# A turn's last twelve probability blocks: from TensorE's transposes to VectorE's 32x32 squares and a way through HBM

## The chip, the core and the metric

The kernel runs on one core of one Trainium2 chip. The metric is the device time of one execution in microseconds; the kernel before was timed in three runs. One further execution was taken with the hardware profiler, and every row below comes from it.

## The reference

One transformer layer with adaptive normalisation, for two sequences of 1024 tokens and 256 features, all in float32:

```
mod = silu(c) @ wmod                                   # shift, gain and gate for both halves
h   = layernorm(x) * (1 + ca) + sa
x   = x + ga * attention(h)       # 16 query heads, 4 key/value heads, 128 features, causal
h   = layernorm(x) * (1 + cb) + sb
x   = x + gb * ffn(h)             # gated (silu), weights behind Walsh-Hadamard transforms
```

Inside the attention: `scores = q k^T / sqrt(128)`, masked where a key lies behind its query, a softmax over the keys, `out = probabilities @ v`, and a projection back to 256 features that is summed over the heads.

## The kernel before

**Two numbers for one.** Every float32 matrix that goes into a matmul is split into a high and a low part, and a product is three matmuls (high x high, high x low, low x high; the helper `three`, L971 to L973). ScalarE makes the high part from PSUM, VectorE subtracts it from the same PSUM bank to get the low part.

**Turns, rows, units.** The attention runs in 8 turns (2 sequences x 4 key/value heads). In a turn there are 8 query rows of 128 tokens, each with 4 heads. Row i needs keys 0 to i, thus i + 1 key blocks of 128. One key block of one row, over the four heads, is a *unit*: 36 in a turn. Rows are paired in four windows of nine units, (7, 0), (6, 1), (5, 2), (4, 3).

**One unit.** `T`: TensorE transposes the probabilities of four heads, 128x128 each, into half of a PSUM tensor (L1097, two such halves); ScalarE copies them to `pt_hi` (L644), VectorE writes `pt_lo` (L869), three slots each. `V`: two units later TensorE multiplies them with the values into the row's output bank (L971 to L973 with `pt_hi`, `pt_lo`, `v_hi`, `v_lo`).

**One row of scores.** `S`, for a row and a head: three matmul passes (L1082, L1085, L1088) into one of two score tensors; VectorE adds the mask and takes the row maximum (L865); ScalarE takes the exponential, with its sum (L619); GpSimd inverts the sum (L511) and scales the row (L514). The scores of a window are made between the units of the window before it, so a row is complete in SBUF several units ahead of its first transpose. TensorE may write a score tensor again when the exponential of two heads before is done.

**The order.** There is no scheduler: `walk()` writes one list of steps, and every engine goes through that list and does its own share, in order. Semaphores order the engines among themselves. Steps besides `T`, `V` and `S` are `C` (a projection chunk of the next turn's q, k, v, in the last window), `Y` (a finished row through the output projection, and VectorE's addition to x, L879), `VT` (the values transposed), `LF`, `LN`, `L`, `LH`, `LL` (the second layer norm of 256 tokens, in the second window), `W` and `WP` (GpSimd's splitting of weights), `B` (butterflies of the down weights, on GpSimd, last turn) and `GB` (the second gate, VectorE, second turn). The projected row of the last window ends inside the next turn.

**DMA.** SP issues all large transfers from one queue, in program order: the weights of each turn (`w_raw`, L422, and `wp_raw`, L413), which wait until the former ones have been split, and at the start the down weights into `raw_down` (L418), which lie there unused until the last turn.

After the attention the feed-forward part runs to the end, with its own loop. The change does not touch it beyond its buffers.

## Time and profile before

| | us |
|---|---|
| median of 3 runs (lowest, highest) | 958.68 (958.41, 958.84) |
| the profiled execution | 958.28 |
| its span, first to last instruction | 956.1 |

| engine | busy us | share of the span | instructions |
|---|---|---|---|
| TensorE, matmuls | 937.3 | 98% | 5504 |
| TensorE, weight loads | 822.0 | 86% | 5504 |
| VectorE | 646.9 | 68% | 1313 |
| ScalarE | 509.1 | 53% | 1062 |
| GpSimd | 455.5 | 48% | 596 |

The span and what lies around it (2.2 us) make the profiled execution's own time. Matmuls are pipelined and a matmul's end is modelled, so the busy time of TensorE is an upper figure; the distance between the starts of neighbours is the safer measure. Idle time of an engine costs only where another one waits for it. Lines are those of the kernel before.

### The profile page before, as it was taken

What the parts mean: (1) busy time and instruction counts of PE and PEld (TensorE: products, weight loads), DVE (VectorE), ACT (ScalarE), POOL (GpSimd) and SP (SyncE); (2) the same over time, 40 slices, a digit from 0 to 9 for tenths busy, and PEclk for the clock granted to TensorE, in tenths of its full rate; (3) what the DMA queues carried; (4) which work ended last, traced back from release to release, by engine and by line L of the source; (5) the groups of instructions that cost most, each with busy time, mean ns of one, the idle gap of its engine ahead of it and who ended that gap; (6) DMA issues with size and microseconds to landing.
All of it is one profiled execution on the core that took longest, in us unless ns stands there. A gap on an engine that the chain in (4) does not pass through costs nothing.

```text
span 956.1 us, 14857 instructions
## 1 busy us (share of the span) xinstructions
PE 937.3 (98%) x5504; PEld 822.0 (86%) x5504; DVE 646.9 (68%) x1313; ACT 509.1 (53%) x1062; POOL 455.5 (48%) x596
## 2 busy tenths in 40 slices
PE   6999999999999999999999999999999999999997
PEld 5889889988998899889888898889888987888887
DVE  5677657766786577657765787478747876874554
ACT  3366556655665566546654666466546665321111
POOL 1466627662766175717670767076707674120000
PEclk9999999999999999999999999999999999999999
DMA  8000100000000000100000000000000011000000
GB/s 316 23 1 2 34 1 23 1 34 1 23 2 34 1 23 1 34 1 23 2 34 1 24 1 34 1 23 2 1 1 1 1 46 55 1 2 22 22 22 22
DMA packets 9603, 21.28 MB, mean 22 GB/s; under 512 B 1216, under 2 KB 5568, under 8 KB 9408
## 3 DMA queue, kind: packets, MB, share of 16 engines
q1 hardware_dynamic: 8816, 20.19, 6.2%
q8 instruction: 41, 0.67, 0.3%
q10 hardware_dynamic: 720, 0.21, 0.1%
q14 instruction: 26, 0.21, 0.1%
HBM read 18.30 MB, written 2.10 MB: 21 GB/s over the span
## 4 chain that ended last, share of the span: by engine, by line
PE 88%; DVE 6%; ACT 4%; DMA 1%; issue 1%; SPq 0%; POOL 0%; DVEq 0%; ACTq 0%; POOLq 0%
PE ps L971 19%; PE ps L973 18%; PE ps L972 18%; PE ps L1097 11%; PE ps L1082 6%; PE ps L1088 6%; PE ps L1085 6%; DVE ps L865 3%; ACT prob L619 2%; DVE pt_lo L869 2%; ACT pt_hi L644 1%; PE ps L995 1%; DMA w_raw<-in_wqkv 1%; PE ps L1051 1%; PE ps L1142 1%
## 5 line engine op out<-in xcount | busy, mean ns | idle before, releaser
L511 POOL TENSOR_TENSOR rinv<-rsum,mone 128x1 f32<-128x1 f32 x256 | 142.8, 558 | 264.8 <-ACT prob L619 264.7
L869 DVE TENSOR_TENSOR pt_lo<-ps,pt_hi 128x512 fp32r<-128x512 f32 x288 | 198.1, 688 | 63.9 <-ACT pt_hi L644 62.1
L644 ACT ACTIVATE pt_hi<-ps 128x512 fp32r<-128x512 f32 x288 | 170.9, 596 | 128.2 <-PE ps L1097 127.3
L619 ACT ACTIVATE prob<-ps,nmax 128x1024 f32<-128x1024 f32 (+7 forms) x256 | 189.7, 741 | 84.8 <-DVE nmax L865 84.0
L865 DVE CUSTOM_DVE_ANT_0 ps<-ps,mask_f 128x1024 f32<-128x1024 f32 (+7 forms) x256 | 193.7, 763 | 46.7 <-PE ps L1088 44.9
L514 POOL TENSOR_SCALAR prob<-prob,rinv 128x1024 f32<-128x1024 f32 (+7 forms) x256 | 191.3, 747 | 54.0 <-POOL rinv L511 54.0
L1097 PE MATMUL ps<-ident,prob 128*128 128x128 f32 x1152 | 172.0, 273 | 0.9 <-POOL prob L514 0.2
L1097 PEld LDWEIGHTS ps<-ident,prob 128*128 128x128 f32 x1152 | 140.9, 140 | 22.8 <-DVE pt_lo L869 2.1
L971 PE MATMUL ps<-pt_hi,v_hi 128*128 128x512 f32 x288 | 134.3, 466 | 0.0
L1082 PE MATMUL ps<-k_hi,q_hi 128*128 128x512 f32 (+4 forms) x384 | 112.7, 347 | 2.7 <-ACT prob L619 2.7
L973 PE MATMUL ps<-pt_hi,v_lo 128*128 128x512 f32 x288 | 113.7, 395 | 0.0
L972 PE MATMUL ps<-pt_lo,v_hi 128*128 128x512 f32 x288 | 113.5, 394 | 0.0
L1088 PE MATMUL ps<-k_hi,q_lo 128*128 128x512 f32 (+4 forms) x384 | 110.6, 342 | 0.0
L1085 PE MATMUL ps<-k_lo,q_hi 128*128 128x512 f32 (+4 forms) x384 | 110.4, 342 | 0.0
L821 DVE SCALAR_TENSOR_TENSOR q_lo<-ps,q_hi 128x512 fp32r<-128x512 f32 x64 | 44.1, 691 | 61.3 <-ACT q_hi L608 61.3
L1082 PEld LDWEIGHTS ps<-k_hi,q_hi 128*128 128x128 f32 x384 | 69.5, 189 | 15.8 <-ACT prob L619 3.5
L971 PE MATMUL ps<-h_hi,w_hi 128*128 128x512 f32 x192 | 78.9, 411 | 2.9 <-DVE h_lo L757 2.9
L608 ACT ACTIVATE q_hi<-ps 128x512 fp32r<-128x512 f32 x64 | 38.3, 598 | 73.4 <-PE ps L973 73.4
L1085 PEld LDWEIGHTS ps<-k_lo,q_hi 128*128 128x128 f32 x384 | 70.7, 188 | 7.7
L973 PE MATMUL ps<-h_hi,w_lo 128*128 128x512 f32 x192 | 75.9, 395 | 0.0
L972 PE MATMUL ps<-h_lo,w_hi 128*128 128x512 f32 x192 | 75.7, 394 | 0.0
L1088 PEld LDWEIGHTS ps<-k_hi,q_lo 128*128 128x128 f32 x384 | 70.4, 188 | 5.2
(137 smaller groups left out, 1685.9 us busy)
## 6 DMA issues: line engine op xcount, KB each, us to landing
w_raw<-in_wqkv SPq DMA_DIRECT2D x8, 768.0 KB, 4.2
wp_raw<-in_wproj SPq DMA_DIRECT2D x8, 512.0 KB, 3.5
prob<-in_wug SPq DMA_DIRECT2D x4, 512.0 KB, 4.6
out_y<-prob SPq DMA_DIRECT2D x8, 256.0 KB, 2.2
x<-in_x SPq DMA_DIRECT2D x3, 512.0 KB, 12.4
prob<-in_wmod SPq DMA_DIRECT2D x1, 1024.0 KB, 10.2
raw_down<-in_wdn SPq DMA_DIRECT2D x1, 1024.0 KB, 13.7
x<-in_x SPq DMA_DIRECT2D x2, 256.0 KB, 4.0
```

The costliest lines, as they stand in the source:

```text
L514: g_.tensor_scalar(row(i, h), row(i, h), rinv[:, at, h:h + 1], 1.0, ALU.mult, ALU.mult).then_inc(prob_done, 1)
L619: a_.activation(row(i, h).rearrange("p (a n) -> p a n", a=nb), score_banks(i, h).rearrange("p (a n) -> p a n", a=nb)[:, :, 0:w], ACT.Exp, ...
L644: a_.activation(pt_hi[:, n % 3, :], ring(t, "T", n), ACT.Copy).then_inc(pth_done, 1)
L865: v_.tensor_tensor_reduce(scores, scores, late, -1.0, 3.0e38, ALU.add, ALU.min, nmax[:, place(n), h:h + 1]).then_inc(max_done, 1)
L869: v_.tensor_tensor(pt_lo[:, n % 3, :], ring(t, "T", n), pt_hi[:, n % 3, :].bitcast(F32), ALU.subtract).then_inc(ptl_done, 1)
L971: mm(dst, w_h, r_h, start=start, stop=False)
L972: mm(dst, w_h, r_l, start=False, stop=False)
L973: return mm(dst, w_l, r_h, start=False, stop=stop)
L1082: mm(dst[:, a * CH:a * CH + wide], q_hi[:, h, q_at], k_hi[:, a * w:a * w + wide], start=True, stop=False)
L1085: mm(dst[:, a * CH:a * CH + wide], q_hi[:, h, q_at], k_lo[:, a * w:a * w + wide], start=False, stop=False)
L1088: last = mm(dst[:, a * CH:a * CH + wide], q_lo[:, h, q_at], k_hi[:, a * w:a * w + wide], start=False, stop=True)
L1097: last = tr(ring(t, "T", n)[:, q * P:(q + 1) * P], row(i, q, j * P, (j + 1) * P), ident[:, :])
```

## The change

Twelve of a full turn's 36 units are no longer transposed by TensorE. They are the last ones of the large rows: key blocks 5 to 7 of row 7, 3 to 6 of row 6, 3 to 5 of row 5, 3 and 4 of row 4. In the last turn only the seven of rows 7 and 6 are moved.

For a moved row there are three new steps:

- `X`, per head: VectorE transposes each 32x32 square of the row's last blocks where it stands, from `prob` into a new tile `blocks` (a STREAM_TRANSPOSE of 128 partitions x 384, 512, 384 or 256 columns).
- After the fourth head SP stores `blocks` in HBM (`spill`, two slots), waits for that, and loads it back in four transfers of 32 partitions into `raw_down`, so that the squares land in their transposed places. `raw_down` holds one row's group: the load waits until the last low part of the former group is made.
- `E`, per unit: ScalarE copies the unit from `raw_down` to `pt_hi`, VectorE writes `pt_lo`, both one unit ahead of where the transpose stood. `V` is as before.

`pt_hi` and `pt_lo` get a fourth slot; the small and the large row of a window are interleaved in another order (`ORDER`), so that moved and transposed units mix; the down weights are loaded in the last turn instead of at the start, and both butterflies stand in the last window. The butterflies' tiles share memory with `blocks`. The splitting of high and low parts stays with ScalarE and VectorE.

```diff
+ORDER = ("bbbsbbxxx", "bbbsxsxxx", "bbbssxsxx", "bbbssxssx")
...
+def moved(t, n):
+    return n in MOVED and (t + 1 < TURNS or UNITS[n][0] > 5)
...
+        turns7 = [(t, "X", NT - 1, h) for h in range(QPG)]
+        out += rest[:1] + [(t, "VT", 0, 0)] + (turns7[2:3] if t else []) + s0[3 if t else 0:] + ([s6[0]] if t else []) + rest[1:]
+        out += [(t, "WP", 0, 0)] + turns7[3:] if t else []
...
+            if t + 1 < TURNS and 0 < p + 1 < NW or t + 1 == TURNS and p == 0:
+                for h, k in enumerate((3, 4, 5, 7) if p == 0 < t else (4, 5, 6, 8) if p == 0 else (3, 4, 5, 6)):
+                    squares[k].append((t, "X", WINDOWS[p + 1][0], h))
+            elif t + 1 < TURNS:
+                squares[7].append((t + 1, "X", NT - 1, 0))
+                squares[8].append((t + 1, "X", NT - 1, 1))
...
+                if n + 1 < NU and moved(t, n + 1):
+                    out.append((t, "E", n + 1, 0))
+                out += extra[:1] + ([] if moved(t, n) else [(t, "T", n, 0)]) + extra[1:]
...
+            def swap_blocks(t, i):
+                g, size = GROUPS.index((t, i)), len(group_units(i))
+                sp.wait_ge(block_done, squared(t, i, QPG - 1))
+                sp.dma_start(spill[g % 2, :, 0:size * CH], blocks[:, 0:size * CH]).then_inc(spill_s[g % 2], 16)
+                sp.wait_ge(*spilled(t, i))
+                if g:
+                    t_of, i_of = GROUPS[g - 1]
+                    sp.wait_ge(el_done, max(entered(t_of, n) for n in MOVED if UNITS[n][0] == i_of))
+                for kb in range(NB):
+                    sp.dma_start(raw_down[kb * QB:(kb + 1) * QB, 0:size * CH].rearrange("p (a n) -> p a n", a=NB),
+                                 spill[g % 2, :, kb * size * P:(kb + 1) * size * P].rearrange(
+                                     "(a p) n -> p a n", a=NB)).then_inc(swap_s[g % 2], 16)
...
+                if what == "E":          # ScalarE
+                    act.wait_ge(pv_done, this(pv_done, t, n - 3))
+                    act.wait_ge(*landed(t, UNITS[n][0]))
+                    a_.activation(by_head(pt_hi, n), swapped_tile(n), ACT.Copy).then_inc(eh_done, 1)
...
+                if what == "E":          # VectorE
+                    dve.wait_ge(eh_done, entered(t, n))
+                    v_.tensor_tensor(by_head(pt_lo, n), swapped_tile(n), by_head(pt_hi, n).bitcast(F32),
+                                     ALU.subtract).then_inc(el_done, 1)
+                if what == "X":
+                    if h == 0 and g:
+                        dve.wait_ge(*spilled(*GROUPS[g - 1]))
+                    dve.wait_ge(prob_done, this(prob_done, t, scored(n, h)))
+                    v_.transpose(blocks[:, 0:len(mine) * CH].rearrange("p (k j h q) -> p j k h q", k=NB, j=len(mine), h=QPG)[:, :, :, h, :],
+                                 row(n, h, mine[0] * P, (n + 1) * P).rearrange("p (j k q) -> p j k q", j=len(mine), k=NB)
+                                 ).then_inc(block_done, 1)
```

The order of VectorE in the first window of the fifth turn, from the low part of the fourth transposed unit on, before (L869 low part, L865 a row maximum, here of row 1's heads, L874 low part of a finished output, L879 addition to x):

```order
L869 TENSOR_TENSOR pt_lo<-ps,pt_hi 128x512 x2
L865 ISA ps,nmax<-ps,mask_f 128x256
L865 ISA nmax 128x1
L869 TENSOR_TENSOR pt_lo<-ps,pt_hi 128x512
L874 TENSOR_TENSOR o_lo<-ps,o_hi 128x512
L865 ISA ps,nmax<-ps,mask_f 128x256
L865 ISA nmax 128x1
L869 TENSOR_TENSOR pt_lo<-ps,pt_hi 128x512
L865 ISA ps,nmax<-ps,mask_f 128x256
L865 ISA nmax 128x1
L869 TENSOR_TENSOR pt_lo<-ps,pt_hi 128x512
L879 TENSOR_TENSOR x<-ps,x 128x256
```

And now (L988, L984, L993 and L998 are the same four; L965 a square transpose of row 6, L958 the low part of a moved unit):

```order
L965 STREAM_TRANSPOSE blocks<-prob 128x4x4x32
L988 TENSOR_TENSOR pt_lo<-ps,pt_hi 128x512
L965 STREAM_TRANSPOSE blocks<-prob 128x4x4x32
L958 TENSOR_TENSOR pt_lo<-raw_down,pt_hi 128x512
L984 ISA ps,nmax<-ps,mask_f 128x256
L984 ISA nmax 128x1
L988 TENSOR_TENSOR pt_lo<-ps,pt_hi 128x512
L993 TENSOR_TENSOR o_lo<-ps,o_hi 128x512
L965 STREAM_TRANSPOSE blocks<-prob 128x4x4x32
L958 TENSOR_TENSOR pt_lo<-raw_down,pt_hi 128x512
L984 ISA ps,nmax<-ps,mask_f 128x256
L984 ISA nmax 128x1
```

Three squares stand there that were not, and the first moved low part stands ahead of a row maximum.

TensorE in the same place, before (L1082 to L1088 scores of row 1, L1097 four transposes, L971 to L973 a unit's product with the values):

```order
L1082 MATMUL ps<-k_hi,q_hi 128x256
L1085 MATMUL ps<-k_lo,q_hi 128x256
L1088 MATMUL ps<-k_hi,q_lo 128x256
L1097 MATMUL ps<-ident,prob 128x128 x4
L971 MATMUL ps<-pt_hi,v_hi 128x512
L972 MATMUL ps<-pt_lo,v_hi 128x512
L973 MATMUL ps<-pt_hi,v_lo 128x512
```

And now (L1201 to L1207 the scores, L1090 to L1092 the product), from the second head's scores on:

```order
L1201 MATMUL ps<-k_hi,q_hi 128x256
L1204 MATMUL ps<-k_lo,q_hi 128x256
L1207 MATMUL ps<-k_hi,q_lo 128x256
L1090 MATMUL ps<-pt_hi,v_hi 128x512
L1091 MATMUL ps<-pt_lo,v_hi 128x512
L1092 MATMUL ps<-pt_hi,v_lo 128x512
```

The four transposes are gone from between them; the sequence score, product comes twice in a row here.

SP's queue at the start and in the first turn, before and then now:

```order
L393 DMA x<-in_x 128x4x256 x2
L418 DMA raw_down<-in_wdn 128x2048
L422 DMA w_raw<-in_wqkv 128x1536 [waits w_ready]
L413 DMA wp_raw<-in_wproj 128x1024 [waits wp_ready]
L422 DMA w_raw<-in_wqkv 128x1536 [waits w_ready]
```

```order
L467 DMA x<-in_x 128x4x256 x2
L494 DMA spill<-blocks 128x1536 [waits blocks_turned]
L500 DMA raw_down<-spill 32x4x384 [waits blocks_spilled0]
L500 DMA raw_down<-spill 32x4x384 x3
L513 DMA w_raw<-in_wqkv 128x1536 [waits w_ready]
L487 DMA wp_raw<-in_wproj 128x1024 [waits wp_ready]
L494 DMA spill<-blocks 128x2048 [waits blocks_turned]
L500 DMA raw_down<-spill 32x4x512 [waits swapped_lo_done,blocks_spilled1]
```

The weights of the next turn now stand behind the swap of row 7's group, and SP waits in this queue for VectorE.

## Rows read from the trace of the kernel before

**Rows 1.** The page, busy us, share of the span, instructions
```profile
PE 937.3 (98%) x5504; PEld 822.0 (86%) x5504; DVE 646.9 (68%) x1313; ACT 509.1 (53%) x1062; POOL 455.5 (48%) x596
```
**Rows 2.** The page, the chain that ended last, share of the span by engine
```profile
PE 88%; DVE 6%; ACT 4%; DMA 1%; issue 1%; SPq 0%; POOL 0%; DVEq 0%; ACTq 0%; POOLq 0%
```
**Rows 3.** Groups by line and shape: busy us, mean ns | idle before, releaser
```profile
L869 DVE TENSOR_TENSOR pt_lo<-ps,pt_hi 128x512 fp32r<-128x512 f32 x288 | 198.1, 688 | 63.9 <-ACT pt_hi L644 62.1
...
L511 POOL TENSOR_TENSOR rinv<-rsum,mone 128x1 f32<-128x1 f32 x256 | 142.8, 558 | 264.8 <-ACT prob L619 264.7
...
L917 DVE TENSOR_TENSOR pt_lo<-prob,pt_hi 128x512 fp32r<-128x512 f32 x32 | 22.2, 693 | 1.1
...
L865 DVE CUSTOM_DVE_ANT_0 ps<-ps,mask_f 128x384 f32<-128x384 f32 x32 | 17.7, 554 | 4.8 <-PE ps L1088 4.8
...
L915 DVE CAST pt_hi<-prob 128x512 fp32r<-128x512 f32 x32 | 13.7, 427 | 1.1
L865 DVE CUSTOM_DVE_ANT_0 ps<-ps,mask_f 128x256 f32<-128x256 f32 x32 | 13.6, 425 | 0.0
```
**Rows 4.** Stretches of the fifth turn: length, then busy us (instructions) by engine
```profile
434.00:531.00 97.00, 96.35 (x575) 84.60 (x574) 66.60 (x136) 57.90 (x124) 53.29 (x72) 1.00 0.05 15
...
448.06:476.40 28.34, 27.69 (x178) 24.86 (x177) 22.15 (x51) 18.85 (x45) 18.02 (x29) 1.00 0.04 14
...
462.30:476.40 14.10, 13.64 (x88) 12.39 (x89) 11.44 (x25) 10.26 (x25) 8.83 (x14) 1.00 0.00 1
484.00:494.40 10.40, 10.40 (x63) 8.88 (x62) 7.57 (x16) 7.05 (x19) 9.34 (x9) 1.00 0.07 14
```
**Rows 5.** TensorE in order of time: start us, duration us, line, operation
```profile
473.83 0.60 PE L1097 MATMUL ps<-ident,prob 128*128 128x128 f32 x4
474.19 0.48 PE L971 MATMUL ps<-pt_hi,v_hi 128*128 128x512 f32 x1
474.50 0.40 PE L972 MATMUL ps<-pt_lo,v_hi 128*128 128x512 f32 x1
...
494.37 0.39 PE L971 MATMUL ps<-h_hi,w_hi 128*128 128x512 f32 x1
494.60 0.40 PE L972 MATMUL ps<-h_lo,w_hi 128*128 128x512 f32 x1
```
**Rows 6.** VectorE in order of time, fifth turn
```profile
439.97 0.42 DVE L879 TENSOR_TENSOR x<-ps,x 128x256 f32<-128x256 f32 x1 [0.21 <-PE ps L973]
...
449.07 0.69 DVE L869 TENSOR_TENSOR pt_lo<-ps,pt_hi 128x512 fp32r<-128x512 f32 x1 [1.11 <-ACT pt_hi L644]
449.68 0.42 DVE L865 CUSTOM_DVE_ANT_0 ps<-ps,mask_f 128x256 f32<-128x256 f32 x1
...
466.75 1.07 DVE L742 TENSOR_SCALAR xhat<-x,mv,rstd 128x256 f32<-128x256 f32 x2
```
**Rows 7.** The chain of waits in order of time, fifth turn: start us, us, what
```profile
441.19 1.10 DVE ps L865
442.34 0.60 DVE pt_lo L869
...
448.55 0.50 ACT pt_hi L644
```
**Rows 8.** DMA issues (KB each, median us to landing), and one issue in SP's timeline
```profile
w_raw<-in_wqkv SPq DMA_DIRECT2D x8, 768.0 KB, 4.2
...
out_y<-prob SPq DMA_DIRECT2D x8, 256.0 KB, 2.2
...
492.47 0.33 SPq L422 DMA_DIRECT2D w_raw<-in_wqkv  x1
```
**Rows 9.** GpSimd and VectorE in order of time, fifth turn and behind the last
```profile
472.89 0.82 POOL L511 TENSOR_TENSOR rinv<-rsum,mone 128x1 f32<-128x1 f32 x1 [0.77 <-ACT prob L619]
...
472.89 0.42 DVE L750 CAST h_hi<-h 128x512 fp32r<-128x512 f32 x1
...
804.84 1.32 POOL L542 TENSOR_SCALAR w_hi<-raw_down 128x1024 fp32r<-128x1024 f32 x1 [8.03 <-PE ps L1143]
```

More of the change, by code:

```diff
@@ L30 @@
 WINDOWS = [(NT - 1 - p, p) for p in range(NW)]
-HEAD = 3
-UNITS = []
-for big, small in WINDOWS:
-    UNITS += [(big, j) for j in range(HEAD)] + [(small, j) for j in range(small + 1)] + [(big, j) for j in range(HEAD, big + 1)]
+ORDER = ("bbbsbbxxx", "bbbsxsxxx", "bbbssxsxx", "bbbssxssx")
+QB = 32
+NB = P // QB
+GROUP = 4
+UNITS, MOVED = [], []
+for (big, small), order in zip(WINDOWS, ORDER):
+    for n, kind in enumerate(order):
+        UNITS.append((small, order[:n].count("s")) if kind == "s" else (big, n - order[:n].count("s")))
+        if kind == "x":
+            MOVED.append(len(UNITS) - 1)
 NU = len(UNITS)
@@ L49, with group_units @@
 LAG = 2
+def moved(t, n):
+    return n in MOVED and (t + 1 < TURNS or UNITS[n][0] > 5)
+def group_units(i):
+    return [j for row, j in (UNITS[n] for n in MOVED) if row == i]
 def chunks(t):
@@ L120, in walk @@
                     fill[k + 3].append((t, "GB", k, 0))
-            if t + 1 == TURNS and p > 1:
-                fill[2].append((t, "B", p - 2, 0))
+            if t + 1 == TURNS and p == 3:
+                fill[0].append((t, "B", 0, 0))
+                fill[4].append((t, "B", 1, 0))
             if t + 1 == TURNS and p == 3:
                 fill[5].append((t, "H", 0, 0))
-            for n, extra in zip(units, fill):
-                out += extra[:1] + [(t, "T", n, 0)] + extra[1:]
+            for n, extra, square in zip(units, fill, squares):
+                if n + 1 < NU and moved(t, n + 1):
+                    out.append((t, "E", n + 1, 0))
+                out += extra[:1] + ([] if moved(t, n) else [(t, "T", n, 0)]) + extra[1:]
                 behind.append(n)
@@ L129, in walk @@
                     value()
+                out += square
         while behind:
@@ L192, in build @@
         raw_down = sb("raw_down", [P, NM * HID])
-        sum_dn, dif_dn = (sb(name, [P, 2, KH, HID])[:, :, :, :] for name in ("sum_down", "dif_down"))
+        blocks = sb("blocks", [P, GROUP * CH])
+        sum_dn, dif_dn = (blocks[:, n * 2 * CH:(n + 1) * 2 * CH].rearrange("p (a k n) -> p a k n", a=2, k=KH) for n in range(2))
         had_r = [sb(f"had_r{n}", [P, 2 * P], F32R)[:, :] for n in range(2)]
@@ L231, in build @@
         wmod_sb = part(1024, KH, 6 * HID)
+        scb = part(1024 + KH * 6 * HID, KH, B, P)
         guard_a, guard_b = sum_dn[:, 0, :, :], sum_dn[:, 1, :, :]
@@ L328, in ring_free @@
             if what == "T":
-                return ptl_done, this(ptl_done, t, n + 1)
+                return ptl_done, transposed(t, n)
             if what == "VT":
@@ L409, in _, with load_wp @@
             sp.dma_start(mask_f[:, :], mask_in).then_inc(small_s, 16)
-            for t in range(TURNS):
+            def load_wp(t):
                 sp.wait_ge(wp_ready, t + 1)
@@ L428, in _ @@
                 done = [m for m, (i, j) in enumerate(UNITS) if window(i) % 2 == n // 2]
-                sp.wait_ge(t_done, this(t_done, TURNS - 1, done[-1] + 1))
+                sp.wait_ge(t_done, transposed(TURNS - 1, done[-1]))
                 sp.dma_start(raw[n], wug[n, :, :].rearrange("p (k n) -> p k n", k=KH)).then_inc(raw_s[n], 16)
@@ L642, in _ @@
                 if what == "T":
-                    act.wait_ge(t_done, this(t_done, t, n + 1))
-                    a_.activation(pt_hi[:, n % 3, :], ring(t, "T", n), ACT.Copy).then_inc(pth_done, 1)
+                    act.wait_ge(t_done, transposed(t, n))
+                    a_.activation(pt_hi[:, n % 4, :], ring(t, "T", n), ACT.Copy).then_inc(pth_done, 1)
+                    exps()
+                if what == "E":
+                    act.wait_ge(pv_done, this(pv_done, t, n - 3))
+                    act.wait_ge(*landed(t, UNITS[n][0]))
+                    a_.activation(by_head(pt_hi, n), swapped_tile(n), ACT.Copy).then_inc(eh_done, 1)
+                    exps()
+                if what == "V" and moved(t, n + LAG):
                     exps()
@@ L1111, in _ @@
                         pe.wait_ge(v_lo_s, this(v_lo_s, t, 2))
-                    pe.wait_ge(ptl_done, this(ptl_done, t, n + 1))
-                    three(O[i], v_hi[:, j, :], v_lo[:, j, :], pt_hi[:, n % 3, :], pt_lo[:, n % 3, :],
+                    if moved(t, n):
+                        pe.wait_ge(el_done, entered(t, n))
+                    else:
+                        pe.wait_ge(ptl_done, transposed(t, n))
+                    three(O[i], v_hi[:, j, :], v_lo[:, j, :], pt_hi[:, n % 4, :], pt_lo[:, n % 4, :],
                           j == 0, j == i).then_inc(pv_done, 1)
@@ L1237 @@
     args.append(nc.dram_tensor("out_y", (B * NT, P, HID), F32, kind="ExternalOutput").ap())
+    args.append(nc.dram_tensor("spill", (2, P, GROUP * CH), F32, kind="Internal").ap())
     build(nc, *args)
```

73 lines of the change are left out of this document (55 added, 18 removed).

## The prediction, made before the changed kernel was run

> **What bounds the kernel now.** I read the page first: TensorE is busy 98% of the 956.1 us span, VectorE 68%, ScalarE 53%, GpSimd 48% [rows 1]. The reader is to see one nearly full engine and one that is two thirds full. The chain of waits says the same: 88% of it is TensorE, 6% VectorE, 4% ScalarE [rows 2]. So what is taken from TensorE is worth its place in TensorE's row, as long as the other engines keep up. The groups by line give durations [rows 3], and one turn, the fifth (t=4), in order of time gives the distances from start to start. Last I read busy time by stretch, since VectorE's average hides an uneven load: over the turn of 97.0 us it is busy 66.60, but 22.15 in the 28.34 us from 448.06, where TensorE already shows small holes (27.69 busy), at a granted clock of 1.00 [rows 4]. In the 14.10 us from 462.30 VectorE is busy 11.44, 81%, the fullest stretch that I found.
>
> **What goes from TensorE.** Seven turns lose 12 of their 36 transposed units, the last turn 7: 7 x 12 + 7 = 91 of 288 units of four transposes. Busy time is no measure of one, as matmuls overlap; starts are. Four transposes start at 473.83 and the next matmul at 474.19: 0.355 us. The matmul behind them pays too: its successor starts 0.31 us later (474.19 to 474.50), where a 128x512 matmul with no transposes in front is followed after 0.23 (494.37 to 494.60) [rows 5]. Together 0.435 us a unit, and 91 x 0.435 = 39.6 us. That is the whole prize: 918.7 us from the profiled execution's 958.3, if all that is added is hidden.
>
> **What VectorE gets.** The low part of a moved unit replaces that of a transposed one. It reads SBUF twice instead of PSUM and SBUF; the row of that kind took 693 ns against 688 [rows 3], so I count it at nothing. New are 16 square transposes in a full turn (4 heads each of row 7 with 384 columns, row 6 with 512, row 5 with 384, row 4 with 256). No row shows one. A pass of VectorE over 512, 384 and 256 columns took 688, 554 and 425 ns [rows 3], of which the last 0.08 overlap the next instruction (449.07 to 449.68 is 0.61 for one of 0.69 [rows 6]): 0.61, 0.48, 0.34 of occupation. I take these, an ordinary pass over a tile: 4 x (0.48 + 0.61 + 0.48 + 0.34) = 7.6 us a turn. Bounds for the same 12 x 512 columns: the CAST of 512 columns at 427 ns gives 5.1 us [rows 3]; two normalisations of 256 columns in 1.07 us, 0.50 each without the tail [rows 6], give 24 x 0.50 = 12.0 us.
>
> The Trainium skill, "VectorE: DVE Perf Modes", section "The three transpose paths", puts a 128x128 bf16 transpose in 32x32 blocks at 311 ns. No run here shows it; if each 128 columns cost that, an estimate is 48 x 0.311 = 14.9 us a turn, and the sum would be about 971.
>
> **Where that hurts.** First stretch, 448.06 to 476.40: seven of the moved units stand in it, so TensorE alone would need 28.34 - 7 x 0.435 = 25.3 us. VectorE gets three squares of row 6 and four of row 5, 3 x 0.61 + 4 x 0.48 = 3.7: 22.15 + 3.7 = 25.9 us [rows 4]. (Busy time counts the tails, so the need may be a microsecond less.) The two are equal, and VectorE becomes the bound of this stretch. The chain into it already runs off TensorE: row maximum, exponential, high part, low part from 441.19 to 449.05 [rows 7]. Both ends: 25.3 if VectorE never idles, 32.0 if it stays at 81% (25.9 / 0.81). I take 27.0, VectorE at 96%, nearer the full end because a moved unit's high part waits for no transpose and four slots instead of three hold the results: 1.3 of 3.05 us kept. Second stretch, 484.00 to 494.40: three units go, TensorE 9.1; VectorE 7.57 + 4 x 0.34 = 8.9 [rows 4]. I take 9.8, VectorE at 91%, since the stretch is short: 0.6 kept. The other two units of a turn stand beside the next turn's projections; outside the two stretches VectorE is busy 66.60 - 22.15 - 7.57 = 36.9 of 58.3 us [rows 4], 63%: 0.9 kept. Row 7's squares fall there too.
>
> **The way through HBM.** Row 7's last square follows the addition at 439.97, so it ends near 439.97 + 0.34 + 0.48 = 440.8 [rows 6]. The store of 768 KB I put at the 4.2 us of the 768 KB load; no row stores that much, but 256 KB to HBM landed in 2.2. The loads back are four issues: 4.2, plus at most three issue times of 0.33 [rows 8]. Trip 8.4 to 9.4, landed at 449.2 to 450.2. ScalarE comes to the first moved high part when that of 448.55 is done, at 449.05 [rows 7], and VectorE, with a square to do behind its low part of 449.07 (to 449.7 + 0.6 = 450.3), needs it then: a wait of 0 to 0.5 us. Row 6's group is 1 MB: by the slope between the 256 and 768 KB rows 1.0 more each way, 10.4 to 11.4 us against some 10 from its last square to the first use: 0 to 1. Behind the waiting high part on ScalarE stand the next high part and the exponentials, and TensorE waits for both. I charge 0.5 us a turn. The groups of rows 5 and 4 have 11 us and more. In the first turn row 7's squares stand behind the second low part; from the end of the first one to the use lie 448.55 - 442.94 = 5.6 us in the turn shown [rows 7], and one row maximum more stands between in turn 0, so about 6.9 against 9.4: 2.5 us once. SP's weight loads now queue behind the swaps and are needed half a turn later: nothing.
>
> GpSimd's normalised rows feed the squares, and the trace shows one cost between the two engines: the reciprocal that started with VectorE's CAST at 472.89 took 0.82 us [rows 9], where L511's mean is 558 ns [rows 3]. The Trainium skill, "GPSIMD Engine Reference", section "Key points", says that GpSimd shares its SBUF interfaces with VectorE; by that rule, with which the 0.82 agrees in kind, the 12 new low parts could hold GpSimd 12 x 0.6 = 7.2 us a turn. GpSimd is busy 53.29 of 97.0 [rows 4], so the sum stays.
>
> The butterflies of the down weights move a window later in the last turn, onto a GpSimd without scores; 8 us of idling lie behind them before it has work again [rows 9]. Nothing.
>
> **Sum.** Turns 0 to 6: 7 x (1.3 + 0.6 + 0.9 - 0.5) = 16.1. Turn 7 (only rows 7 and 6 move, three squares in the first stretch: VectorE 22.15 + 1.8 = 24.0 under TensorE's 25.3, at 92% 26.1): 2.2 - 0.5 = 1.7. First turn -2.5. Net 15.3 of the 39.6 us: 943.0 for a profiled execution; the median of the runs lies 0.4 above that one, which I leave in the rounding: 943.
>
> **Rivals.**
> (1) All hidden. For: over a turn VectorE would be at 66.6 + 7.6 = 74.2 of 91.8 us; 25.9 is overstated by tails. Against: the holes TensorE has already. 958.3 - 39.6 + 2.5 = 921.
> (2) Squares at the upper price, 12.0 us a turn. First stretch (22.15 + 5.8) / 0.96 = 29.1, 0.8 more than before; second (7.57 + 2.15) / 0.96 = 10.1, 0.3 kept; with 0.9 - 0.5 that is 0.1 lost a turn; with the first turn's 2.5 and turn 7's gain of 1.5: 960. The 2.4 us a turn lost for 4.4 put the point where it turns slower near 11.5. The page on the transpose paths speaks for this one, and by its figure for more.
> (3) The way through HBM is later: the one that ends slower by one mechanism. Place: the first moved high part after the groups of rows 7 and 6, where ScalarE, then VectorE, then TensorE stop. Each microsecond beyond 9.4 and 11.4 costs 2 a turn, 16 in all, so it decides from 1.1 us on. For: a store of this size and short runs back are in no row. Against: 4.2 us for 768 KB. At 2 us late: 975.
> (4) Coupling: VectorE stays at 81% because each of its instructions waits for another engine. 32.0 instead of 28.3 in the first stretch, 3.7 lost, 0.6 + 0.9 - 0.5 kept: 2.7 lost a turn, 19; turn 7 (24.0 / 0.81 = 29.6) 1.8, the first turn 2.5: 981 at that end. At 90% (28.8) it gains 3.
>
> **Numbers.** Forecast 0.45 (own range 934 to 952), (1) 0.17, (2) 0.13, (3) 0.13, (4) 0.12. A difference of 0.2%, 1.9 us, is what a measurement here can tell. Faster: 0.45 + 0.17 + 0.04 of (2) + 0.04 of (4) = 0.70; slower 0.24; same 0.06. Range 920 to 968: (1) and (2) whole, the near parts of (3) and (4).
>
> **What would show it.** Squares that occupy 0.61, 0.48, 0.34; in the first stretch VectorE over 90% busy and TensorE waiting for low parts or exponentials; a turn of 94.7 us (97.0 - 2.3), not 91.8 and not 97; a wait for the load back under 1 us, largest in the first turn. It is wrong if TensorE stays at 98% (1), if a square of 512 columns lasts over 0.9 us (2), if ScalarE's longest waits name the loads (3), or if VectorE is still near 81% while the turn grows (4).

## The result and the profile after

The changed kernel takes 1086.93 us (median of 4 runs, 1084.77 to 1088.85), the kernel before 958.72 beside it: a ratio of 1.1337, 95% interval 1.1313 to 1.1361. The forecast was 943, its range 920 to 968; no rival came near either, the slowest of them stood at 981.

The page of the changed kernel, whose second line answers to [rows 1] and whose third to [rows 2]:

```profile
span 1087.1 us, 14544 instructions
...
PE 954.5 (88%) x5140; PEld 813.6 (75%) x5140; DVE 707.2 (65%) x1433; ACT 515.5 (47%) x1062; POOL 472.5 (43%) x596
...
PE 47%; DVE 23%; DMA 14%; ACT 8%; issue 6%; SPq 2%; POOL 0%; DVEq 0%; ACTq 0%; POOLq 0%
...
L988 DVE TENSOR_TENSOR pt_lo<-ps,pt_hi 128x512 fp32r<-128x512 f32 x197 | 135.2, 687 | 35.0 <-ACT pt_hi L742 33.8
...
L958 DVE TENSOR_TENSOR pt_lo<-raw_down,pt_hi 128x512 fp32r<-128x512 f32 x91 | 76.7, 843 | 89.0 <-ACT pt_hi L747 89.0
...
spill<-blocks SPq DMA_DIRECT2D x15, 768.0 KB, 3.3
raw_down<-spill SPq DMA_DIRECT2D x60, 192.0 KB, 4.2
```

The reader is to see three things. No engine is full any more: TensorE has 364 matmuls fewer and is 88% busy, VectorE 65%. The chain that was 88% TensorE is 47% TensorE, and VectorE, the DMAs and ScalarE hold nearly all the rest: the kernel is now bound by a sequence, not by an engine. And there are two kinds of low part: L988 reads PSUM and takes 687 ns, as before [rows 3]; L958 reads SBUF twice, takes 843 on average, and VectorE stood idle for 89.0 us in front of it, waiting for ScalarE's high part. The squares are about the size that was forecast: 568, 702 and 431 ns for 384, 512 and 256 columns, against 554, 688 and 425.

A turn, and three stretches of 7 us near and in it (length, then busy us of TensorE, its weight loads, VectorE, ScalarE and GpSimd, granted clock, DMA share, GB/s), against the 97.0 us and the clock of 1.00 in [rows 4]:

```profile
513.52:626.20 112.68, 98.89 (x529) 84.21 (x528) 74.31 (x152) 58.94 (x125) 56.24 (x71) 0.94 0.23 68
```
```profile
505.00:512.00 7.00, 6.94 (x50) 6.26 (x49) 5.09 (x16) 3.68 (x13) 4.32 (x8) 1.00 0.00 0
519.00:526.00 7.00, 4.66 (x29) 3.81 (x27) 5.21 (x10) 3.54 (x9) 4.82 (x7) 1.00 0.93 274
...
575.00:582.00 7.00, 3.81 (x10) 2.68 (x11) 3.46 (x8) 2.56 (x6) 6.17 (x9) 0.66 0.38 136
```

The stretch with no moved unit (505) is as good as before. Where row 7's group is awaited (519) TensorE is busy 4.7 of 7 us. The stretch from 575 stands right behind the place where a weight step of GpSimd (570.76 to 574.27) met a moved low part (572.91 to 574.82): TensorE pauses for 2.2 and for 2.1 us, is busy 3.8 of 7 us, and the granted clock is 0.66, a mixture of the chip's two levels. At the lower one, matmuls of 512 columns start 0.43 us apart (580.14, 580.57, 580.99) where they start 0.23 to 0.24 apart at the upper.

The chain of the changed kernel in order of time (start us, us, what), over three moved units; "issue" is time in which the engine, here ScalarE, waits for nothing that the profile shows:

```profile
549.20 0.69 DVE pt_lo L958
549.89 0.47 DVE ps L984
550.60 0.34 issue
550.94 0.19 ACT prob L717
551.14 0.91 ACT h L682 x2
552.05 0.53 ACT pt_hi L747
552.60 0.69 DVE pt_lo L958
553.29 0.47 DVE ps L984
553.89 0.46 issue
554.34 0.19 ACT prob L717
554.53 0.53 ACT pt_hi L747
555.09 0.69 DVE pt_lo L958
```

This is the mechanism in one piece. Low part, row maximum, exponential, next high part, next low part: a closed loop over VectorE and ScalarE, once for each of the moved units here, 2.49 us from 552.60 to 555.09 and 3.40 from 549.20 to 552.60, where 0.91 us of ScalarE's layer norm stands in between. No TensorE instruction stands in it. The high part takes a slot of `pt_hi` that a value step must have left, but that is not what it waits for: 2.3 us, once, in the whole trace, against 33.6 for the loads. The loop comes from where the entry of unit n+1 was put: ahead of the score step of unit n, so VectorE makes the low part before the maximum and ScalarE the next high part behind the exponential that waits for this maximum. A transposed unit stands behind its score step: the high part needs only TensorE, and the next maximum does not stand behind a low part that waits for an exponential. Within one unit the round closes where a moved unit follows a moved one, five times in a full turn (the neighbouring `x` in `ORDER`); at the others a transposed unit lies between.

### The profile page after: what moved, and what is told of

It is laid out like the page before. It is cut to its first block, busy times and chain, and to the rows that moved or that the text cites. A ratio compares the mean times of both kernels' runs of the same rounds, so it can differ in the third digit from the quotient of the medians.

```text
span 1087.1 us, 14544 instructions
## 1 busy us (share of the span) xinstructions
PE 954.5 (88%) x5140; PEld 813.6 (75%) x5140; DVE 707.2 (65%) x1433; ACT 515.5 (47%) x1062; POOL 472.5 (43%) x596
## 4 chain that ended last, share of the span: by engine, by line
PE 47%; DVE 23%; DMA 14%; ACT 8%; issue 6%; SPq 2%; POOL 0%; DVEq 0%; ACTq 0%; POOLq 0%
PE ps L1090 13%; PE ps L1092 12%; PE ps L1091 12%; DMA raw_down<-spill 8%; DVE ps L984 6%; DVE pt_lo L958 6%; DMA spill<-blocks 6%; PE ps L1216 3%; ACT pt_hi L747 3%; DVE blocks L965 3%; ACT prob L717 2%; PE ps L1201 2%; PE ps L1207 2%; SPq L500 2%; PE ps L1204 2%
## 5 line engine op out<-in xcount | busy, mean ns | idle before, releaser
L612 POOL TENSOR_SCALAR prob<-prob,rinv 128x1024 f32<-128x1024 f32 (+7 forms) x256 | 203.9, 796 | 54.0 <-POOL rinv L609 54.0
L984 DVE CUSTOM_DVE_ANT_0 ps<-ps,mask_f 128x1024 f32<-128x1024 f32 (+7 forms) x256 | 192.4, 758 | 25.9 <-PE ps L1207 25.6
L1090 PE MATMUL ps<-pt_hi,v_hi 128*128 128x512 f32 x288 | 133.6, 464 | 43.2 <-DVE pt_lo L988 42.5
L988 DVE TENSOR_TENSOR pt_lo<-ps,pt_hi 128x512 fp32r<-128x512 f32 x197 | 135.2, 687 | 35.0 <-ACT pt_hi L742 33.8
L1201 PE MATMUL ps<-k_hi,q_hi 128*128 128x512 f32 (+4 forms) x384 | 117.4, 360 | 44.6 <-ACT prob L717 44.5
L742 ACT ACTIVATE pt_hi<-ps 128x512 fp32r<-128x512 f32 x197 | 117.1, 594 | 68.0 <-PE ps L1216 67.6
L958 DVE TENSOR_TENSOR pt_lo<-raw_down,pt_hi 128x512 fp32r<-128x512 f32 x91 | 76.7, 843 | 89.0 <-ACT pt_hi L747 89.0
L1216 PE MATMUL ps<-ident,prob 128*128 128x128 f32 x788 | 124.1, 284 | 0.8 <-DVE pt_lo L988 0.6
L1201 PEld LDWEIGHTS ps<-k_hi,q_hi 128*128 128x128 f32 x384 | 69.4, 192 | 67.3 <-ACT prob L717 56.8
L1092 PE MATMUL ps<-pt_hi,v_lo 128*128 128x512 f32 x288 | 116.2, 403 | 0.0
L1216 PEld LDWEIGHTS ps<-ident,prob 128*128 128x128 f32 x788 | 102.6, 147 | 17.6 <-issue 1.4
L1207 PE MATMUL ps<-k_hi,q_lo 128*128 128x512 f32 (+4 forms) x384 | 112.4, 347 | 0.0
L1090 PE MATMUL ps<-h_hi,w_hi 128*128 128x512 f32 x192 | 85.8, 447 | 16.8 <-issue 13.9
L1090 PEld LDWEIGHTS ps<-pt_hi,v_hi 128*128 128x128 f32 x288 | 56.3, 196 | 55.3 <-DVE pt_lo L988 52.7
L1090 PE MATMUL ps<-wp_hi,o_hi 128*128 128x256 f32 x256 | 77.3, 302 | 13.4 <-DVE o_lo L993 13.0
L1091 PE MATMUL ps<-h_lo,w_hi 128*128 128x512 f32 x192 | 80.6, 420 | 0.0
L1092 PE MATMUL ps<-h_hi,w_lo 128*128 128x512 f32 x192 | 80.4, 419 | 0.0
```

The lines of the kernel that those rows point to most:

```text
L612: g_.tensor_scalar(row(i, h), row(i, h), rinv[:, at, h:h + 1], 1.0, ALU.mult, ALU.mult).then_inc(prob_done, 1)
L958: v_.tensor_tensor(by_head(pt_lo, n), swapped_tile(n), by_head(pt_hi, n).bitcast(F32), ALU.subtract).then_inc(el_done, 1)
L984: v_.tensor_tensor_reduce(scores, scores, late, -1.0, 3.0e38, ALU.add, ALU.min, nmax[:, place(n), h:h + 1]).then_inc(max_done, 1)
L988: v_.tensor_tensor(pt_lo[:, n % 4, :], ring(t, "T", n), pt_hi[:, n % 4, :].bitcast(F32), ALU.subtract).then_inc(ptl_done, 1)
L1090: mm(dst, w_h, r_h, start=start, stop=False)
L1091: mm(dst, w_h, r_l, start=False, stop=False)
```

## The experiments

Where a kernel reads the down weights in place of the probabilities, or has transposes missing, its numbers mean nothing; the work per instruction is the same. The "source" is the tile from which a moved unit's high and low parts are read.

**1. The new order alone.** `return False` for `moved`, no squares, no groups.

```
-    return n in MOVED and (t + 1 < TURNS or UNITS[n][0] > 5)
+    return False
...
-                    squares[k].append((t, "X", WINDOWS[p + 1][0], h))
+                    pass
```


> Only the new order of units, the fourth slot and the later butterflies are kept; no unit is moved, all 288 are transposed, and no square or transfer is there (down weights loaded at the start as before). If the loss comes from the moved units themselves (theories A, B and C below all say so): within 5 us of before, 954 to 964. If the new order or the shared buffers carry part of it: above 970.

Measured 960.46, ratio 1.0018 (1.0007 to 1.0029). The new order of units, the fourth slot and the late butterflies cost 1.7 to 2 us, where the forecast had nothing.

**2. The change without the trip.** No store, no load back, and none of the waits for them.

```
             def swap_blocks(t, i):
+                return
...
-                    act.wait_ge(*landed(t, UNITS[n][0]))
```


> The changed kernel without its stores to HBM and loads back: the moved units' high and low parts read raw_down, which holds the down weights, so nothing waits for a transfer (the attention's result is meaningless). Theory A (the late trip is the cause: ScalarE waited 33.6 us for it in 15 places, TensorE stands and its clock falls): 960 to 1000. Theory B (a serial loop: the moved unit's high part stands behind the exponential on ScalarE and its low part ahead of the row maximum on VectorE, one round a unit instead of one in two): only the waits and their clock go, 1030 to 1050.

Measured 1059.03, ratio 1.1049 (1.096 to 1.1137), of only two runs that lie 7 us apart; it is above both ranges that were expected. The way through HBM accounts for some 28 of the 128 us; 100 stay with no store and no load at all.

**3 and 4. The entry behind the score step and the transposed unit,** complete (3) and without the trip (4).

```
-                if n + 1 < NU and moved(t, n + 1):
-                    out.append((t, "E", n + 1, 0))
-                out += extra[:1] + ([] if moved(t, n) else [(t, "T", n, 0)]) + extra[1:]
+                enter = [(t, "E", n + 1, 0)] if n + 1 < NU and moved(t, n + 1) else []
+                out += extra[:1] + ([] if moved(t, n) else [(t, "T", n, 0)]) + enter + extra[1:]
```


> The changed kernel with one edit: a moved unit's high and low parts stand behind the score step (and the transposed unit) instead of ahead of it, so VectorE takes the row maximum first. The trip gets later use by a unit as well. Theory B: 1000 to 1040. Theory A: the use is only some 1.5 us later, of 2 us of waiting, so 1045 to 1065. If neither: 1080 or more.

> e2 and e3 together: no transfer to wait for, and the high and low parts behind the score step. If A and B are all of it: at or below before, 925 to 960. If a third cause (C: VectorE's low parts with two SBUF inputs stall beside GpSimd, and the squares fill VectorE) is large: 970 to 1010.

Measured 1063.84, ratio 1.1099 (1.1043 to 1.1155), and 1048.47, ratio 1.0939 (1.0907 to 1.0971): 23 and 11 us back, little. Kernel 3 fell into the range put down for the trip alone, kernel 4 above all of its ranges, so these two by themselves speak against the loop as the whole cause. What their order leaves: both parts are still a unit ahead, the high part mostly behind an exponential, the low part ahead of the next maximum, and VectorE still waits for moved high parts (53.2 us in kernel 3, the lines are under 8). How much of it is the loop entered at another point was not measured.

**5 to 7. A ladder from the new order.** One thing is changed at a time, at the place of a transposed unit: three of the four transposes of the 91 units gone (5, the first fence), the 120 squares added (6), both parts read from SBUF (7, the second fence).

```
-                    for q in range(QPG):
+                    for q in range(QPG - 1 if gone(t, n) else 0, QPG):
```
```
+                        a_.activation(by_head(pt_hi, n), swapped_tile(n), ACT.Copy).then_inc(pth_done, 1)
...
+                        v_.tensor_tensor(by_head(pt_lo, n), swapped_tile(n), by_head(pt_hi, n).bitcast(F32),
+                                         ALU.subtract).then_inc(ptl_done, 1)
```


> e1 (new order, nothing moved) with one edit: for the units that the change moves, TensorE makes one transpose of the four and the other three are left out; ScalarE and VectorE do all that they did, in the same places and from the same PSUM bank, no squares, no transfers (three quarters of those probabilities are stale). It shows what TensorE's saving is worth by itself: 91 x 0.27 us = 24 us. If it is all on the path: 936. If VectorE and ScalarE hold TensorE as soon as its stream gets shorter (theory B', the slack of two units is used up): 950 or more.

> e5 with the 120 square transposes on VectorE in their places. If VectorE's load is what matters (7.6 us a turn at 0.96 full, as the forecast had it): e5 plus 10 to 20. If squares hide: e5 plus 0 to 5. If they are the third cause of e4's 90 us: e5 plus 40 or more.

> e6 with the moved units' high and low parts read from raw_down in SBUF (holding the down weights) instead of from PSUM, still in the place of the transposed unit. Theory C (low parts with two SBUF inputs stall beside GpSimd: mean 843 ns in the changed kernel, 920 in e4, against 688): e6 plus 15 to 40. If only the place in the queues matters (B): e6 plus 0 to 8, and e2 at 1059 owes the rest to standing ahead of the score step.

Measured 940.62, ratio 0.9814 (0.9786 to 0.9843); 956.83, ratio 0.9981 (0.997 to 0.9993); 979.59, ratio 1.0221 (1.0191 to 1.0251). So three quarters of the transposes are worth 19.8 us, the squares take 16.2 of it back, and the source in SBUF costs 22.8, which the forecast had at nothing.

**8. Only the low part moved,** in the complete change: ScalarE's high part where it was, VectorE's behind the score step.

```
+                enter = [(t, "F", n + 1, 0)] if n + 1 < NU and moved(t, n + 1) else []
...
-                if what == "E":
+                if what == "F":
```


> The changed kernel, complete, with one edit: ScalarE makes a moved unit's high part where it did, ahead of the score step, but VectorE makes the low part behind the score step and the transposed unit. Theory B: this breaks the loop of one round a unit on both sides, so clearly under e3's 1064: 1010 to 1045. If B is not the cause: 1060 to 1085.

Measured 1022.59, ratio 1.0669 (1.0609 to 1.073): 64 us back. The second line is VectorE's only. VectorE's order is now the same as in kernel 3, and the two kernels differ by 41 us in nothing but the place of ScalarE's high part. VectorE's wait in front of the moved low parts, in the change, in kernel 3 and in kernel 8 (engine line waited for: us in total, times, longest):

```profile
DVE pt_lo L958 <- ACT pt_hi L747: 89.0, 69, 5.1
```
```profile
DVE pt_lo L957 <- ACT pt_hi L746: 53.2, 60, 4.7
```
```profile
DVE pt_lo L959 <- ACT pt_hi L748: 1.6, 8, 0.2
```

So the loop needs both: a low part early in VectorE's order, and a high part late in ScalarE's.

**9 and 10. Both parts at the unit's own place,** complete (9) and without the trip (10). The order is then that of a transposed unit.

```
-                if n + 1 < NU and moved(t, n + 1):
-                    out.append((t, "E", n + 1, 0))
-                out += extra[:1] + ([] if moved(t, n) else [(t, "T", n, 0)]) + extra[1:]
+                out += extra[:1] + [(t, "E" if moved(t, n) else "T", n, 0)] + extra[1:]
```


> The complete change with one thing different: both parts of a moved unit are made at the unit's own place in the order, where the transposes and the copies of another unit stand, behind its score step. Its high part then stands ahead of that step's exponential on ScalarE and its low part behind the row maximum on VectorE, as for a transposed unit. Theory B (the loop high part, low part, row maximum, exponential, next high part, once a unit, is what costs): near the run that read SBUF at that place (979.6) less the remaining single transposes (91 x 0.435 / 4 = 10 us) plus what the trip costs, since it has one unit more of time here: 965 to 985. Rival (the trip through HBM is the main cost): above 1020. Rival (the port contention is the main cost, wherever the parts stand): about the 1048 to 1064 of the orders with both parts a unit ahead.

> As the kernel before it in this list, but no group is stored or loaded: the high and low parts read the down weights, which lie in the same tile (wrong numbers, the same shapes and instructions). Theory B: 960 to 975, the trip worth under 10 us in this order, against 28 (1087 - 1059) where the parts stand ahead of the row maximum. Rival (the trip costs the same wherever the parts stand): 28 less than the complete one.

Measured 987.05, ratio 1.0299 (1.0259 to 1.0339), and 982.43, ratio 1.0265 (1.0236 to 1.0294). Kernel 9 is just above its expected range, kernel 10 7 us above its own. The place alone is worth 100 us of the 128 in the complete kernel and 77 without the trip (1059.03 to 982.43). And the trip, 28 us where a loop stands behind it, costs 4.6 at the own place, with runs that overlap (982.64 to 990.78, 981.55 to 987.74). The same 5140 matmuls keep TensorE busy for less time, as the page of kernel 9 shows beside the 954.5 above, at a mean granted clock of 0.993 for 0.949: so some 32 of the 100 us lay in slower matmuls, which stood behind the pauses.

```profile
PE 922.7 (94%) x5140; PEld 783.2 (80%) x5140; DVE 719.0 (73%) x1433; ACT 509.1 (52%) x1062; POOL 473.9 (48%) x596
...
PE 57%; DVE 24%; ACT 9%; DMA 6%; issue 4%; SPq 1%; DVEq 0%; ACTq 0%
```

**11 and 12. The low part on GpSimd,** at the own place (11) and a unit ahead (12).

```
+                if what == "E":          # GpSimd
+                    pool.wait_ge(eh_done, entered(t, n))
+                    g_.tensor_tensor(by_head(pt_lo, n), swapped_tile(n), by_head(pt_hi, n).bitcast(F32),
+                                     ALU.subtract).then_inc(el_done, 1)
...
-                if what == "E":          # VectorE
```


> Complete, both parts at the unit's own place, but the low part is made by GpSimd instead of VectorE. Theory C (a VectorE instruction that reads SBUF twice is slowed beside GpSimd, some 23 us over the 91 units) with VectorE relieved of 12 x 0.61 us a turn: about 20 to 30 less than with the low part on VectorE, 940 to 960, if GpSimd makes one in 1.3 us and the value step is not waiting for it. Rival (GpSimd, whose normalised rows feed everything, becomes late by 12 x 1.3 = 16 us a turn in the full stretches): equal or more, 975 to 1000.

> As the one before, but both parts stand a unit ahead, behind the score step and the transposed unit of the unit before, so that the low part on GpSimd has one unit more of time. Theory B: ScalarE's high part then stands behind the previous exponential, but the loop is cut, because VectorE's row maximum does not stand behind the low part: 940 to 970, within 10 of the one before. Rival (any high part behind the exponential costs, since TensorE waits for the copies of the transposed unit): 10 to 30 more than the one before.

Measured 1077.79, ratio 1.126 (1.123 to 1.1289), and 1020.69, ratio 1.066 (1.0635 to 1.0686). Both expectations failed. The waits of kernel 11 (engine line waited for: us in total, times, longest):

```profile
POOL rinv L607 <- ACT prob L719: 271.2, 90, 24.2
...
PE ps L1088 <- POOL pt_lo L619: 105.1, 51, 5.0
```

The instruction took 1.27 us (median), about what I had put down, and GpSimd is 53% busy, so it has time enough. But there the low part stands behind a normalisation that waits for the exponential of the same unit. GpSimd waited as long for exponentials before (264.8 us in [rows 3]); what is new is that a low part stands behind such a wait. So TensorE's value step waits for a chain it never depended on: 105.1 us. It is the change's own error in another engine's row. A unit ahead there is more slack: that wait is 56.5 us in kernel 12, and the time is 57 us less. That the order of GpSimd is the cause is read from these waits, no run moved it alone.

**13 and 14. What in SBUF costs the 23 us:** kernel 7 with the low part from PSUM again (13, the fence against kernel 7), and with both parts from SBUF in plain runs of 512 instead of 32 (14).

```
-                        v_.tensor_tensor(by_head(pt_lo, n), swapped_tile(n), by_head(pt_hi, n).bitcast(F32),
+                        v_.tensor_tensor(pt_lo[:, n % 4, :], ring(t, "T", n), pt_hi[:, n % 4, :].bitcast(F32),
```


> The seventh run with one thing taken back: ScalarE's high part still reads the down weights in SBUF, VectorE's low part reads PSUM again (numbers without meaning, as there). Theory C (two operands in SBUF, of an instruction of VectorE, are what costs): low parts at 0.69 us again and the time of the sixth run, 955 to 960. Rival (the high part from SBUF, or its wait, makes the 23 us): 970 to 980.

> The seventh run with both parts on SBUF, but in plain runs of 512 elements instead of runs of 32 taken head by head. Theory C: nothing changes, 975 to 982, mean low part 0.95 to 1.05 us. Rival (the short runs of the swapped layout cost): low parts at 0.69 us and 955 to 962.

Measured 957.84, ratio 0.9987 (0.9977 to 0.9997), and 981.43, ratio 1.0228 (1.0211 to 1.0245). It is the second SBUF operand of VectorE's instruction, not the short runs and not ScalarE's source. The durations of the 91 low parts (ns min/median/max) of kernels 13 and 7:

```profile
L999 DVE TENSOR_TENSOR pt_lo<-ps,pt_hi x91: 679/686/694, 67.1 to 766.3; 128x512 fp32r<-128x512 f32 x91
```
```profile
L999 DVE TENSOR_TENSOR pt_lo<-raw_down,pt_hi x91: 678/694/3870, 65.4 to 787.3; 128x512 fp32r<-128x512 f32 x91
```

The median is unchanged; a few are very long, seven of them 3.56 to 3.87 us, one a turn. VectorE and GpSimd of kernel 7 at one of them, in order of time:

```profile
502.33 3.57 DVE L999 TENSOR_TENSOR pt_lo<-raw_down,pt_hi 128x512 fp32r<-128x512 f32 x1
505.82 0.43 DVE L974 STREAM_TRANSPOSE blocks<-prob 128x256 f32<-128x256 f32 x1
```
```profile
501.86 3.49 POOL L632 TENSOR_TENSOR w_lo<-w_raw,w_hi 128x1536 fp32r<-128x1536 f32 x1
505.30 1.01 POOL L614 TENSOR_TENSOR rinv<-rsum,mone 128x1 f32<-128x1 f32 x1
```

GpSimd's subtraction, which had started first, ends at 505.35, the low part at 505.90: 0.55 us later, a little less than its own length alone. From its start at 502.33 it stood still until GpSimd's was done. The reciprocal behind, which now meets the low part, takes 1.01 us for [rows 3]'s 558 ns. A mean of 1023 hides this; the three numbers of the tile's view show it.

**15 and 16. GpSimd's weight step three units earlier,** in kernel 7 (15) and in the complete kernel 9 (16).

```
-                fill[3].append((t, "W", 0, 0))
+                fill[0].append((t, "W", 0, 0))
```


> The seventh run with one GpSimd step moved: high and low part of the next turn's weights (1.5 and 3.5 us once a turn) stand three units earlier, where VectorE makes no low part from SBUF. Lock (a VectorE instruction with two operands in SBUF and a GpSimd instruction exclude each other for their whole length): the seven low parts of 3.56 to 3.87 us are gone, mean near 0.80 us instead of 1.02, and the time falls by up to 7 x 2.9 = 20 us, less what TensorE had hidden: 963 to 972. Rival (the long ones only meet a late engine, or bandwidth is shared): the mean and the time stay, 977 to 982. Rival (five microseconds more in front of the normalisations of that window): 975 or more with a mean near 0.80.

> The complete kernel of the ninth run (both parts at the unit's own place) with the same GpSimd step three units earlier: 987 less the same 8 to 16 us, 970 to 979; still slower than the kernel before, because 16 us of squares and the short collisions stay. Rival (not the collisions): 984 to 989.

Measured 959.84, ratio 1.0014 (1.0004 to 1.0023), and 961.5, ratio 1.0031 (1.0019 to 1.0042). Both are better than expected: 19.8 of the 22.8 us of the source, and 25.6 of the complete kernel's, were this one meeting a turn, with what the pauses behind it cost (the mean granted clock goes from 0.996 to 0.999 and from 0.993 to 0.999). The low parts of kernel 15:

```profile
L999 DVE TENSOR_TENSOR pt_lo<-raw_down,pt_hi x91: 676/692/1368, 65.5 to 766.6; 128x512 fp32r<-128x512 f32 x91
```

Kernel 16 is the best complete version that the runs point to. It is 125 us faster than the change with two edits to the order and none to the work, and still 3 us slower than before.

**17 and 18. The squares of row 5 later,** in kernel 16, by two units (17) and by two to three (18, with `(6, 7, 7, 8)`), for the stretch from 466.1 to 475.4 us, in which its VectorE had next to no idle time.

```
-                for h, k in enumerate((3, 4, 5, 7) if p == 0 < t else (4, 5, 6, 8) if p == 0 else (3, 4, 5, 6)):
+                for h, k in enumerate((3, 4, 5, 7) if p == 0 < t else (4, 5, 6, 8) if p == 0 else (5, 6, 7, 8) if p == 1 else (3, 4, 5, 6)):
```


> The complete kernel of the sixteenth run with the four squares of row 5 two units later (behind the sixth to ninth unit of their window instead of the fourth to seventh). Theory (VectorE is the bound in that stretch): TensorE's stop of 1.35 us a turn goes and 3 to 9 us come back: 953 to 958.5, perhaps below the kernel before. Rival (the hole only moves to the next stretch, or the squares' load is spread evenly already): 960 to 963. The row group still has about 9 us for its trip against 9 needed.

> The same with the squares behind the seventh, eighth, eighth and ninth unit. If VectorE's load in the stretch is the bound, the same or up to 3 us better than the run before it in this list; if the trip becomes late, worse by up to 1 us a turn, with ScalarE's waits for the loads above the 11 us of the ninth run.

Measured 966.71, ratio 1.0086 (1.0072 to 1.0099), and 967.11, ratio 1.0089 (1.0075 to 1.0103): 5 us worse, where 3 to 9 better was expected. ScalarE's waits for the loads are as in kernel 9 (11.2 and 11.8 us in all), so the trip is not late. The hole only moves: in the fifth turn of kernels 16 and 17, from one value step of TensorE to the next (units counted from 0 in the order of the turn), unit 14 falls from 2.31 to 1.67 us, while unit 17 grows from 2.01 to 2.76 and unit 24 from 6.03 to 6.34. That is 0.5 us a turn; the profiled execution of 17 was also its fastest (963.63), and the rest of the 5 us was not traced. No version that beats the kernel before was found.

## Why the prediction was wrong, point by point

The ladder gives the sum that the forecast should have had, each term the difference of two medians: order 960.46 - 958.72 = 1.7; three of four transposes -19.8; squares 16.2; source in SBUF 22.8; both parts a unit ahead, with the last transposes gone, 1059.03 - 979.59 = 79.4; trip 1086.93 - 1059.03 = 27.9. Together 128.2, the whole difference. (It is a ladder: another order of the steps would share the amounts differently, as the trip's 28 and 4.6 show. The last two terms hang on kernel 2, whose two runs lie 3.5 us on either side of the median.)

- **What goes from TensorE: nearly right.** Forecast 0.435 us a unit. For three quarters of the transposes, with the pair of matmuls behind them still paying for a start, 91 x 0.355 x 3/4 = 24 were to come; 19.8 did. The fourth transpose bought nothing that I could see: kernel 10 has none and stands 2.8 us above kernel 7. Whether the prize of 39.6 was ever whole stays open.
- **What VectorE gets: right in size.** An ordinary pass over a tile was the right price (0.57, 0.70, 0.43 us), and of the prize the forecast gave back 39.6 - 7 x 2.8 - 2.2 = 17.8 us for VectorE's load; the squares cost 16.2. The upper price of rival 2 is refuted by the trace. So is the estimate of 14.9 us a turn, worked out from the 311 ns that the Trainium skill gives in "VectorE: DVE Perf Modes", section "The three transpose paths", for 128x128 bf16: 4 x (0.57 + 0.70 + 0.57 + 0.43) = 9.1 us of busy time, tails included.
- **The step that failed: "nearer the full end because a moved unit's high part waits for no transpose".** What the high part does not wait for was counted, what it stands behind was not. On ScalarE it stood behind an exponential, on VectorE the low part stood before a maximum, and together they closed the loop above: 2.49 us against TensorE's 1.24 for such a unit (473.19 to 474.43 in kernel 16). Kernels 2 and 10 show 77 us for the place of both parts; in the complete kernel 8 gives back 64 for the low part's place, and 9 another 36 for both at the unit's own. The rounds that close within one unit, five in a full turn and four in the last, do not add up to that: 39 of them in all turns are 39 x 1.25 = 49 us. In the fifth turn, by TensorE's value steps, kernel 2 is 9.6 us longer than kernel 10: 2.5, 3.6, 2.9 and 0.6 in the four windows, which have 3, 4, 3 and 2 moved units. So the cost goes with the moved units, and the waits at the transposed ones beside them are part of it. The forecast's first stretch tells what the step was worth. From the value step of unit 3 to that of unit 16 it was 29.2 us before and 34.9 in the change, with VectorE 69% busy, not 96%; in kernel 16, with the parts at their own place, it is 27.0, with VectorE 88% busy. Rival 4, coupling, had the right kind, "each of its instructions waits for another engine", but priced it by the old trace's 81%, which was that of the old order. VectorE went to 66% over the turn.
- **"reads SBUF twice ... so I count it at nothing": failed, 23 us.** The row of 693 ns [rows 3] is the same form of instruction, but all 32 of them stand at 812 us and later, behind the last turn, where GpSimd is busy 10.4 of 136 us; what I took for the price of the form was its price without a neighbour. The trace showed the cost between the two engines (0.82 us at 472.89, [rows 9]), and I asked only what it could do to GpSimd. The Trainium skill, "SBUF — State Buffer", section "SBUF: two separate sides", says it outright: of a VectorE instruction with two inputs in SBUF and a GpSimd one that reads SBUF, the one that starts first holds a shared pair of ports for its whole length, and the other is blocked. The trace agrees: 3.57 us behind the start of one of 3.49. With that rule the forecast could have asked which GpSimd instruction is the longest and who stands beside it; the answer is one instruction a turn. The 23 us are its price at the unit's own place (kernel 7). In the change's own order the seven longest moved low parts took 1.90 to 2.66 us, so there it was less, and what it was worth there no run shows.
- **The way through HBM: lengths nearly right, price wrong.** Row 7's group took 10.0 us from the end of its last square to the high part that waited for it (513.51 to 523.52), forecast 8.4 to 9.4; row 6's 11.2 for 10.4 to 11.4. The charge of 0.5 us a turn, with the first turn's 2.5 us 6.5 in all, fits the 4.6 of the own place. In the change's order it was 3.5 a turn: the first use stood a unit earlier, everything of the next unit stood behind it, and the clock fell behind such pauses. Kernel by kernel the same wait has two prices. The row 7 trip as the chain shows it:

```profile
513.01 0.50 DVE blocks L965
513.52 3.25 DMA spill<-blocks
516.79 0.30 SPq L500
...
518.09 5.35 DMA raw_down<-spill
...
523.52 0.64 ACT pt_hi L747
```

- **The butterflies and the order of units, "nothing":** 1.7 us.
- **The clock: absent from the forecast.** It was 1.00 in every row read, so every lost microsecond was counted once. Its mean was 0.949 after, 0.993 in kernel 9, 0.999 in kernel 16.

## What to carry to other kernels

When a step is put elsewhere in an order that all engines follow, write down for each engine what it now stands behind and ahead of, and follow that round until it ends at TensorE or closes on itself; a closed loop has a length, and that length against the bound engine's share of it is a term of the forecast, which may be too low, since the units beside the loop wait too. A duration is a property of an instruction and its neighbour: before taking one from a row, look where in the span the row stands and what runs beside it there, and read minimum, median and maximum, not the mean. And a wait is priced by what stands behind it.

## What the runs showed of the hardware that was not expected

- VectorE with two operands in SBUF stood still until a GpSimd instruction of 3.49 us, begun 0.47 us before it, was done (low part 3.57 us, median 694 ns); with one operand in PSUM, in the program that differs in that alone, all 91 lay between 679 and 694 ns. GpSimd is held in turn: its scaling of 512 columns took 805 ns in kernel 7, 698 in kernel 6.
- A float32 transpose in 32x32 squares costs what a pass over the tile costs: 568 ns for 384 columns, 702 for 512, 431 for 256.
- Behind two pauses of TensorE, of 2.2 and 2.1 us (573.9 to 579.15), stood a stretch at the lower clock (starts 0.43 us apart for 0.24), so that a wait was paid for again in the time after it; with the same matmuls TensorE was busy 954.5 us in one order and 922.7 in another.
- Four loads of 192 KB issued one behind the other hold SP's queue for 1.73 us, and the weight loads that now follow them took 6.9 and 7.5 us to land where it was 4.2 [rows 8] and 3.5 before. No wait for them is in the trace: the one wait for weights, 8.0 us, stands at 11.4 us, before the first swap.
